# Two transformer layers on one core: the values' split moves to GpSimd, and the accumulator, the query copies and the casts of the second attention are laid out anew

## The chip, the cores and the metric

One Trainium2 chip, one of its cores. The metric is the device time in microseconds (us) of one execution of the whole kernel.

## The reference

Two adaLN blocks run one after the other on x of 2 batches x 512 rows x 512 columns, in fp32. Layer 0 is a sliding window attention with 32 query and 8 key heads and a merged low-rank projection. Layer 1 is the part that matters here: attention with 128 heads of 4 content columns each and a rotary part of 64 columns, then a base projection with 8 low-rank experts.

```python
q_c = (c_q @ Wq_up).reshape(b, s, 128, 4)
q_r = (x @ Wq_rope).reshape(b, s, 128, 64)
k_c = (c_kv @ Wk_up).reshape(b, s, 128, 4)
v_c = (c_kv @ Wv_up).reshape(b, s, 128, 4)
k_r = x @ Wk_rope
scores = (einsum('bqhd,bkhd->bhqk', q_c, k_c) + einsum('bqhd,bkd->bhqk', q_r, k_r)) / scale
attn = softmax(scores, axis=-1)
out = einsum('bhqk,bkhd->bqhd', attn, v_c).reshape(b, s, 512) @ Wo
```

## The kernel before

The five engines run programs written out by hand, which meet only at semaphores. In the second attention the work is cut into 128 **units**: 64 pairs of heads times 2 batches. An even unit is batch 0 of a pair, the odd unit behind it is batch 1 of the same pair. All engines go through **turns** (`period` on ScalarE, VectorE and SyncE, `before_sums` and `behind_sums` on TensorE, `turn` on GpSimd). What one turn u does, in TensorE's order:

- scores 0 to 3 of unit u (two matmuls each, L2551 and L2558), with the maxima products 0 and 1 of unit u+2 between them (L2538)
- `sum_unit(u - 1)`: probabilities times values of the unit before, into bank 7
- scores 4 to 7 of unit u, maxima products 2 to 7 of unit u+2, and the rotary queries of unit u+3 (12 matmuls, L2468 to L2470)

The sums come in two forms. For units below `HALVED` (104) both factors are 16-bit: every probability tile of 128x512 is cast to fp16 and the rest is taken in a second fp16 tile (`halved_part(..., 0)` and `(..., 1)`), and the values are split in three bf16 parts. For three of four key tiles this gives 12 matmuls of 32 columns (L2575), the fourth tile stays fp32 (L2580). From unit 104 on the sums are 8 fp32 matmuls (L2585); this form is called direct here.

What the other engines do in a turn:

- **ScalarE**: the rotary queries' high part from PSUM into `q2` (L1325, L1326), 8 exponentials (L1368), the fp16 casts of tiles 2 to 5 (L1372, L1378), one copy of bank 7 into `ost` (L1364), and the copy of `q2`'s rotary rows into `q1` (`q_high_again`, L1332, L1333).
- **GpSimd** (`halve`): the fp16 casts of tiles 0 and 1 (L879), the six subtractions for the second fp16 tiles, here called the lows (L881, L891), and in every even turn the low part of the rotary weights (L828) between lows 1 and 2.
- **VectorE**: the low part of the rotary queries (L1841, L1842), 8 maxima (L1896), their transpose into `mrow` (L1906), in every even turn the high part of the rotary weights (L1762), and `values`: five small operations on 8 or 24 elements a partition (L1869 to L1878) that split the next unit's values into `vp`.
- **SyncE** issues all transfers of a turn in one fixed order: keys for unit u+1 (L562), keys for the maxima of unit u+3 (L569), content queries of unit u+3 (L573), in even turns rotary weights (L522), four stores of `ost` into `o_d` (L596), and, once VectorE's transpose is there, two small copies of `mrow` into `q2` (L604). Each begins with `hold`, a wait for a semaphore. TensorE's first maxima product of a unit waits for the transfers of L569 and L573 (`mc_loaded`).

SyncE's, ScalarE's, VectorE's and GpSimd's turns run in loops of four turns (`LOOP`, up to turn 101) and are written out before and behind them. TensorE's sums of a unit wait for `p_split` (all six lows), `vp_ready` (the values) and `o_copied` (bank 7 is free).

Of the kernel before, what the change touches and what calls it, by code (L numbers as in the profile page):

```python
# [15 lines left out]
P = 128  # L16
# [19 lines left out]
EARLY = B * (KT - 1)  # L36
TAIL = UNITS - 22
HALVED = TAIL - 2
LOOP = (HALVED - 4) // 4 * 4 + 2
# [5 lines left out]
OROWS = 4 * HD1  # L45
CR = 4 * HD1
SLOTS = [(0, 0), (0, 1), (1, 0), (1, 1), (0, 2), (1, 2), (0, 3), (1, 3)]
HTILES = 3
CONTENT_DMAS = (16, 32)
# [20 lines left out]
def adaln_two_layers(nc, a, out):  # L70
# [4 lines left out]
    o_d = scratch("o_d", (B, H1, 2, OROWS, S))  # L75
# [3 lines left out]
    with ctx:  # L79
# [252 lines left out]
        f_loaded, last_added, f_er_mm, f_er, f_as, fbias_loaded = (sem(n) for n in ("f_loaded", "last_added", "f_er_mm", "f_er", "f_as", "fbias_loaded"))  # L332
# [8 lines left out]
        qr_mm, q2_hi, q1_hi, q1_split = sem("qr_mm"), sem("q2_hi"), sem("q1_hi"), sem("q1_split")  # L341
# [84 lines left out]

        @block.sync
        def _(sp):
# [63 lines left out]
            for k in range(KT):  # L492
# [7 lines left out]
                         .rearrange("p o n -> p (o n)")).then_inc(fbias_loaded, 16)  # L500
# [55 lines left out]
            def period(u, k):  # L556
# [26 lines left out]
                if exists(v, UNITS):  # L583
                    vb = (k + 1) % 2
                    hold(o_copied, v + 1)
                    if not exists(v, DIRECT):
                        for h in range(2):
                            at = HD1 * (2 * (v // 2) + h - H1 + 32)
                            for par in range(2):
                                for dst, r in zip(SUMS[vb], (0, DEN)):  # L590
                                    r += 64 * h + 32 * par
                                    sp.dma_start(dst[at:at + HD1, par], ost[r:r + HD1, vb]).then_inc(sums_loaded[vb], 16)
                    for h in range(2 if exists(v, DIRECT) else 0):
                        for par in range(2):
                            j = 2 * h + par
                            sp.dma_start(o_d[vb, hd(u, k, -1, h), par].rearrange("o c s -> (o c) s"), ost[32 * j:32 * j + OROWS, (k + 1) % 2])\  # L596
                              .then_inc(o_stored[(k + 1) % 2], 16)

                v = u + 2
                if exists(v, UNITS):  # L600
                    hold(m_turned, v + 1)
                    for h in range(2):
                        r = maxrow(h)
                        sp.dma_start(q2[r:r + 1, (k + 2) % 4, h].bitcast(F32).rearrange("p (q n) -> p q n", q=4),  # L604
                                     mrow[h:P:32, k % 2]).then_inc(m_loaded[k % 2], 16)

# [33 lines left out]
            def load_last_sums(b):  # L640

                heads = range(H1 - 32, 2 * (DIRECT // 2))
                sp.wait_ge(o_stored[b], 64 * (DIRECT // 2))
                sp.wait_ge(oo_split, EARLY - 1 + b)
                for par in range(2):
                    for dst, r in zip(SUMS[b], (0, DEN)):
                        sp.dma_start(dst[0:HD1 * len(heads), par], o_d[b, heads.start:heads.stop, par, r:r + HD1]).then_inc(sums_loaded[b], 16)
# [27 lines left out]
            sp.wait_ge(o_copied, UNITS)  # L675
# [22 lines left out]
        def _(pool):  # L698
# [131 lines left out]
            def zero_others():  # L830
# [6 lines left out]
                pool.memset(vp[:, :, HTILES:TB, :, DEN:DEN + HD1], 1.0).then_inc(zeroed, 1)  # L837
                pool.memset(vpb[:, :, 0:HTILES, :, DEN:DEN + HD1], 1.0).then_inc(zeroed, 1)

# [32 lines left out]
            content_low(3)  # L872
            def halve(u, k, pair):

                par = k % 2
                for i in range(2):
                    pool.wait_ge(exp1, 8 * u + 5 + i)
                    pool.sem_inc(spare, 1)
                    pool.tensor_copy(halved_part(par, i, 0), PT[par][:, i]).then_inc(p_split, 1)  # L879
                    pool.wait_ge(p_split, 4 * u + i + 1)  # L880
                    e = pool.tensor_tensor(halved_part(par, i, 1), PT[par][:, i], halved_part(par, i, 0), ALU.subtract)  # L881
                    if i == 1:
                        e.then_inc(p_split, 1)
                if k % 2 == 0:
                    split_rope_weights(pair(4), (k // 2) % 2)
                for i in range(2, 2 * HTILES):
                    if i > 2:
                        pool.wait_ge(exp1, 8 * u + 6 + i)
                    else:
                        pool.wait_ge(exp1, 8 * u + 9)  # L890
                    e = pool.tensor_tensor(halved_part(par, i, 1), PT[par][:, i], halved_part(par, i, 0), ALU.subtract)  # L891
                e.then_inc(p_split, 1)
# [4 lines left out]

            for u in range(6):
                turn(u, u % 4, lambda n, u=u: (u + n) // 2)
# [6 lines left out]
            def load_sums(n, par):  # L906

                b, m = n % 2, n // 2
                if par == 0 and n < B:
                    pool.wait_ge(o_stored[b], 64 * (PAIRS - PAIRS // KT))  # L910
                if par == 0:
                    wait(pool, oo_split, n - 1)
                    wait(pool, o_added, ADDS * n)
                for dst, r in zip(SUMS[b], (0, DEN)):
                    pool.dma_start(dst[:, par], o_d[b, 32 * m:32 * m + 32, par, r:r + HD1]).then_inc(parts_loaded, 16)
                for i in (1, 2):
                    pool.dma_start(sum_parts[2 * par + i - 1], o_d[b, 32 * m:32 * m + 32, par, i * HD1:i * HD1 + HD1]
# [125 lines left out]
        def _(act):  # L1043
# [284 lines left out]
            def q_high_again(z, k):  # L1328

                if exists(z, UNITS):  # L1330
                    act.wait_ge(q2_hi, z + 1)
# [1546 lines left out]
```

## Time and profile before

| what | value |
|---|---|
| three runs | 2184.45, 2190.09, 2193.27 us |
| median | 2190.09 us |
| the profiled execution, its own time | 2190.74 us |
| span of its trace | 2188.9 us |
| mean granted clock of TensorE | 0.995 |
| second attention, turns 6 to 102, a turn | 9.98 us |
| its direct form, a turn | 10.45 us |

The span is the time from the first to the last instruction. A turn's length is the distance from one transpose (L1906) to the next. In the timelines all times are microseconds from the span's start, and a row that ends in "x2" merges two neighbouring instructions, whose starts are closer than their durations where the engine overlaps them.

### The profile page before, as it was taken

The numbers are of one execution on the slowest core, as the hardware profiler recorded it, in microseconds if no ns is written. First come the engines' busy times: TensorE is split into PE (matmuls) and PEld (weight loads), VectorE is DVE, ScalarE is ACT, GpSimd is POOL, SyncE is SP. The second block draws the span as 40 slices with busy tenths as digits, with TensorE's granted clock in tenths as the row PEclk, the third lists the DMA queues.
The fourth block names the chain that finished last, engine by engine and source line by source line (L and its number), as shares of the span: only waits on it lengthen the run. The fifth ranks groups of instructions, "written<-read, shape, count | busy, mean of one in ns | idle before, by whom it ended". The sixth has DMA issues, their size and how long they took to land.

```text
span 2188.9 us, 43788 instructions
## 1 busy us (share of the span) xinstructions
PE 2135.0 (98%) x11308; PEld 1644.0 (75%) x11308; DVE 1814.7 (83%) x3415; ACT 1535.5 (70%) x3060; POOL 1554.4 (71%) x1395
## 2 busy tenths in 40 slices
PE   7999999999999999999999999999999999999978
PEld 4788888888886757777777777777777777777756
DVE  6787787787786758999999999999999998788764
ACT  2443443443434579999999999999999999777742
POOL 4766766766753448888888888889888988455334
PEclk9999999999999999999999999999999999999999
DMA  7011010010013242111111111111111111433341
GB/s 248 24 45 30 20 47 29 19 48 29 19 26 114 56 159 86 47 49 41 49 47 42 48 48 46 42 48 47 49 42 49 47 48 45 124 97 107 86 127 39
DMA packets 125559, 132.17 MB, mean 60 GB/s; under 512 B 33221, under 2 KB 75877, under 8 KB 125492
## 3 DMA queue, kind: packets, MB, share of 16 engines
q1 hardware_dynamic: 121652, 118.77, 18.4%
q0 software_dynamic: 3840, 12.59, 1.9%
q8 instruction: 33, 0.54, 0.1%
q14 instruction: 34, 0.28, 0.0%
HBM read 101.52 MB, written 29.10 MB: 60 GB/s over the span
## 4 chain that ended last, share of the span: by engine, by line
PE 81%; DVE 9%; issue 4%; SPq 2%; DMA 1%; ACT 1%; POOL 1%; DVEq 0%; ACTq 0%; POOLq 0%
PE bank L2538 10%; PE bank L2551 10%; PE bank L2558 9%; PE bank L2115 7%; PE bank L2117 7%; PE bank L2116 7%; PE bank L2470 5%; PE bank L2468 5%; PE bank L2469 5%; PE bank L2575 3%; PE bank L2585 2%; PE bank L2580 2%; DVE mcol L1896 1%; DVE rope_b L1585 1%; DVE rope_a L1584 1%
## 5 line engine op out<-in xcount | busy, mean ns | idle before, releaser
L1896 DVE TENSOR_REDUCE mcol<-bank 128x1 fp32r<-128x512 f32 x1024 | 690.0, 685 | 118.2 <-PE bank L2538 104.8
L2538 PE MATMUL bank<-km,q 128*128 128x512 f32 x1024 | 417.8, 409 | 5.0 <-ACT q L1326 1.6
L2551 PE MATMUL bank<-q,k 128*128 128x512 f32 x1024 | 417.9, 408 | 0.1
L2558 PE MATMUL bank<-q,k 128*128 128x512 f32 x1024 | 404.2, 395 | 0.0
L2538 PEld LDWEIGHTS bank<-km,q 128*128 128x128 f32 x1024 | 317.6, 310 | 71.6 <-DVE mcol L1896 20.3
L1368 ACT ACTIVATE pT<-bank 128x512 f32<-128x512 f32 x512 | 279.5, 599 | 27.6 <-PE bank L2558 23.1
L1368 ACT ACTIVATE x<-bank 128x512 f32<-128x512 f32 x512 | 279.2, 599 | 23.2 <-PE bank L2558 19.0
L2551 PEld LDWEIGHTS bank<-q,k 128*128 128x128 f32 x1024 | 192.3, 188 | 81.8 <-issue 30.2
L2558 PEld LDWEIGHTS bank<-q,k 128*128 128x128 f32 x1024 | 193.5, 189 | 32.3
L2470 PE MATMUL bank<-hT_hi,wr_lo 128*128 128x512 f32 x512 | 205.3, 401 | 0.0
L2468 PE MATMUL bank<-hT_hi,wr_hi 128*128 128x512 f32 x512 | 202.2, 395 | 0.1
L2469 PE MATMUL bank<-hT_lo,wr_hi 128*128 128x512 f32 x512 | 202.3, 395 | 0.0
L2115 PE MATMUL bank<-hT_hi,w_hi 128*128 128x512 f32 x376 | 150.3, 400 | 0.0
L2117 PE MATMUL bank<-hT_hi,w_lo 128*128 128x512 f32 x376 | 148.5, 395 | 0.0
L2116 PE MATMUL bank<-hT_lo,w_hi 128*128 128x512 f32 x376 | 148.4, 395 | 0.0
L722 POOL TENSOR_TENSOR bq_lo<-rope_a,bq_hi 128x512 fp32r<-128x512 f32 x64 | 83.3, 1302 | 82.0 <-ACT bq_hi L1097 82.0
L881 POOL TENSOR_TENSOR pH<-x,pH 128x512 f16<-128x512 f32 x104 | 131.9, 1269 | 8.3
L714 POOL TENSOR_TENSOR rope_a<-rope_a,rope_b 128x512 f32<-128x512 f32 x80 | 106.0, 1325 | 43.4 <-DVE rope_b L1586 43.4
L891 POOL TENSOR_TENSOR pH_late<-pT,pH_late 128x512 f16<-128x512 f32 x104 | 121.6, 1169 | 19.9 <-ACT pT L1368 18.5
L881 POOL TENSOR_TENSOR pH<-pT,pH 128x512 f16<-128x512 f32 x104 | 121.4, 1167 | 8.3
L828 POOL TENSOR_TENSOR wr_lo<-wst,wr_hi 128x512 fp32r<-128x512 f32 x64 | 82.8, 1293 | 56.1 <-DVE wr_hi L1762 56.0
L891 POOL TENSOR_TENSOR pH<-pT,pH 128x512 f16<-128x512 f32 x104 | 119.5, 1170 | 0.3 <-ACT pT L1368 0.2
(375 smaller groups left out, 5402.4 us busy)
## 6 DMA issues: line engine op xcount, KB each, us to landing
wst<-in_L_attn_Wq_rope SPq DMA_DIRECT2D x64, 256.0 KB, 3.0
o_d<-ost SPq DMA_DIRECT2D x504, 32.0 KB, 1.8
st_q<-in_L_attn_wq SPq DMA_DIRECT2D x8, 1024.0 KB, 7.8
st_wo<-in_L_attn_wo SPq DMA_DIRECT2D x8, 1024.0 KB, 5.1
km<-kc_d SPq DMA_DIRECT2D x256, 32.0 KB
q<-qc_d SPq DMA_DIRECT2D x256, 32.0 KB
k<-kc_d SPq DMA_DIRECT2D x256, 32.0 KB
wm<-in_L_wmod SPq DMA_DIRECT2D x6, 1024.0 KB, 10.2
```

The source lines that it names most:

```text
L881: e = pool.tensor_tensor(halved_part(par, i, 1), PT[par][:, i], halved_part(par, i, 0), ALU.subtract)
L1368: act.activation(PT[k % 2][:, s], bank[s % 4][:], ACT.Exp, scale=float((HD1 + ROPE) ** -0.5)).then_inc(exp1, 1)
L1896: dve.tensor_reduce(mcol[:, k % 2, i % 4, i // 4:i // 4 + 1], bank[4 + i % 2][:], AX.X, ALU.max, negate=True)\
L2115: pe.matmul(ps, lh_, rh, start=(i == 0), stop=False)
L2116: pe.matmul(ps, lh_, rl, start=False, stop=False)
L2117: e = pe.matmul(ps, ll, rh, start=False, stop=(i == n - 1))
L2468: pe.matmul(bank[6][:], wr_hi[:, par, kk], hT_hi[:, kk, at], start=(kk == 0), stop=False)
L2469: pe.matmul(bank[6][:], wr_hi[:, par, kk], hT_lo[:, kk, at], start=False, stop=False)
L2470: e = pe.matmul(bank[6][:], wr_lo[:, par, kk], hT_hi[:, kk, at], start=False, stop=(kk == KT - 1))
L2538: pe.matmul(bank[4 + i % 2][:], q2[:, k % 4, h, i % 4:S:4], km[:, b, h], start=True, stop=True).then_inc(max_mm, 1)
L2551: pe.matmul(bank[s % 4][:], k1[:, k % 2, t], q1[:, k % 4, h], start=True, stop=False)
L2558: pe.matmul(bank[s % 4][:], k2[:, k % 2, h, t], q2[:, k % 4, h], start=False, stop=True).then_inc(scores1, 1)
```

## The change

- `values` runs on GpSimd for the units in the 16-bit form: its five operations stand in `halve` between the rotary weights' low part and lows 2 to 5, and each of the last three waits for the one before. VectorE keeps `values` for the direct form alone.
- All six fp16 casts are ScalarE's. `CAST_BEHIND` says behind which exponential each stands: tile 0 behind exponential 1, tile 1 behind 2, tiles 2 and 3 behind 3, tile 4 behind 4, tile 5 behind 5. GpSimd's lows 0 and 1 now wait for exponentials 2 and 3.
- The values of batch 1 stand 16 columns further in `vp`, so that both batches' sums gather in bank 7. It is copied and stored once for a pair (`o_d` has another layout), with one transfer of 128 rows in place of eight of 16 rows.
- `q_high_again` is gone. SyncE copies the rotary rows of `q2` into `q1` by two transfers of 64 rows x 2 KB, issued behind the two of `mrow` and ahead of the next turn's keys.
- `HALVED` is 96, not 104, and `LOOP` 94, not 102: eight more units take the direct form.
- The bias of layer 0 counts on `f_loaded` (10 transfers, not 9).

```diff
+HALVED = EARLY * UNITS // (B * KT)
+LOOP = HALVED - 2
-HALVED = TAIL - 2
-LOOP = (HALVED - 4) // 4 * 4 + 2
+CAST_BEHIND = {1: (0,), 2: (1,), 3: (2, 3), 4: (4,), 5: (5,)}
...
SyncE, period
-                if exists(v, UNITS):
-                    hold(o_copied, v + 1)
...
-                            sp.dma_start(o_d[vb, hd(u, k, -1, h), par].rearrange("o c s -> (o c) s"), ost[32 * j:32 * j + OROWS, (k + 1) % 2])\
+                if exists(v, DIRECT) and k % 2 == 0:
+                    par, pair = (k - 1) // 2 % 2, pairs(u, k, -1)
+                    hold(o_copied, pair + 1)
+                    sp.dma_start(o_d[bass.ds(pair, 1)].rearrange("o h g b c s -> (o h g b c) s"), ost[:, par]).then_inc(o_stored[par], 16)
...
+                    hold(q2_hi, v + 1)
+                    for h in range(2):
+                        r = slice(ROPE * h, ROPE * h + ROPE)
+                        sp.dma_start(q1[r, (k + 2) % 4, h].bitcast(F32), q2[r, (k + 2) % 4, h].bitcast(F32)).then_inc(q1_hi[k % 2], 16)
...
GpSimd
+            def values(v, k, pair):
+                kp = k % 2
+                full = vc[:, TB * kp:TB * kp + TB, bass.ds(pair * 8, 8)].rearrange("p t (h d) -> p t h d", h=2)
+                src = full[:, 0:HTILES]
+                first, second, third = (vpb[:, kp, 0:HTILES, :, OROWS * kp + i * HD1:OROWS * kp + i * HD1 + HD1] for i in range(3))
+                wait(pool, pv1, v - 1)
+                pool.sem_inc(spare, 1)
+                pool.tensor_copy(first, src).then_inc(vp_ready, 1)
+                pool.tensor_copy(vp[:, kp, HTILES:TB, :, OROWS * kp:OROWS * kp + HD1], full[:, HTILES:TB])
+                pool.wait_ge(vp_ready, VP_STEPS * v + 1)
+                pool.sem_inc(spare, 1)
+                pool.tensor_tensor(vrest, src, first, ALU.subtract).then_inc(vp_ready, 1)
+                pool.wait_ge(vp_ready, VP_STEPS * v + 2)
+                pool.sem_inc(spare, 1)
+                pool.tensor_copy(second, vrest).then_inc(vp_ready, 1)
+                pool.wait_ge(vp_ready, VP_STEPS * v + 3)
+                pool.sem_inc(spare, 1)
+                pool.tensor_tensor(third, vrest, second, ALU.subtract).then_inc(vp_ready, 1)
...
-                    pool.tensor_copy(halved_part(par, i, 0), PT[par][:, i]).then_inc(p_split, 1)
...
+                def lows(tiles):
+                    for i in tiles:
+                        pool.wait_ge(exp1, 8 * u + (7, 8, 9, 9, 10, 11)[i])
+                        pool.sem_inc(spare, 1)
+                        e = pool.tensor_tensor(halved_part(par, i, 1), PT[par][:, i], halved_part(par, i, 0), ALU.subtract)
...
+                lows((0, 1))
                 if k % 2 == 0:
                     split_rope_weights(pair(4), (k // 2) % 2)
+                if not (isinstance(u, int) and u == HALVED - 1):
+                    values(u + 1, k + 1, pair(1))
+                lows(range(2, 2 * HTILES))
...
ScalarE
-            def q_high_again(z, k):
...
-                        if exists(u - 1, UNITS):
+                        if exists(u - 1, UNITS) and (k % 2 == 0 or isinstance(u, int) and u - 1 == DIRECT):
...
+                    if s in CAST_BEHIND and exists(u, HALVED):
...
+                        for i in CAST_BEHIND[s]:
+                            act.wait_ge(exp1, 8 * u + 5 + i)
+                            act.activation(halved_part(k % 2, i, 0), PT[k % 2][:, i], ACT.Copy)
...
TensorE, sum_unit
+                    opens, closes = apart or k % 2 == 0, apart or k % 2 == 1
-                                              start=(kb == 0), stop=False)
+                                              start=(kb == 0 and opens), stop=False)
```

## Rows read from the trace of the kernel before

**Rows 1.** The page, part 1: busy time of each engine.

```profile
PE 2135.0 (98%) x11308; PEld 1644.0 (75%) x11308; DVE 1814.7 (83%) x3415; ACT 1535.5 (70%) x3060; POOL 1554.4 (71%) x1395
```

**Rows 2.** One line (L1906), 870 to 1840 us and 1870 to 2080 us: count, min/median/max ns, first and last start.

```profile
L1906 DVE STREAM_TRANSPOSE mrow<-mcol x97: 406/412/424, 876.2 to 1834.1; 128x128 f32<-128x128 f32 x97
...
L1906 DVE STREAM_TRANSPOSE mrow<-mcol x20: 402/410/417, 1873.7 to 2072.3; 128x128 f32<-128x128 f32 x20
```

**Rows 3.** Timeline of TensorE, even turn 62: start, duration, instruction.

```profile
1436.74 0.40 PE L2538 MATMUL bank<-km,q 128*128 128x512 f32 x1
...
1437.54 0.62 PE L2575 MATMUL bank<-pH,vp 128*32 128x512 f16 x8
...
1444.66 0.40 PE L2538 MATMUL bank<-km,q 128*128 128x512 f32 x1
...
1446.52 0.52 PE L2538 MATMUL bank<-km,q 128*128 128x512 f32 x1
...
1456.48 0.62 PE L2538 MATMUL bank<-km,q 128*128 128x512 f32 x1
```

**Rows 4.** Timeline of ScalarE, the same turn.

```profile
1436.31 2.07 ACT L1368 ACTIVATE x<-bank 128x512 f32<-128x512 f32 x4
1438.41 1.15 ACT L1372 ACTIVATE pH<-x 128x512 f16<-128x512 f32 x2
...
1442.29 0.62 ACT L1332 ACTIVATE q<-q 64x512 fp32r<-64x512 f32 x1
```

**Rows 5.** Timeline of GpSimd, the same turn.

```profile
1437.07 0.61 POOL L879 CAST pH<-x 128x512 f16<-128x512 f32 x1 [1.44 <-ACT x L1368]
1437.77 1.16 POOL L881 TENSOR_TENSOR pH<-x,pH 128x512 f16<-128x512 f32 x1
...
1439.56 1.44 POOL L881 TENSOR_TENSOR pH<-x,pH 128x512 f16<-128x512 f32 x1
1440.96 1.29 POOL L828 TENSOR_TENSOR wr_lo<-wst,wr_hi 128x512 fp32r<-128x512 f32 x1
1442.22 2.30 POOL L891 TENSOR_TENSOR pH<-x,pH 128x512 f16<-128x512 f32 x2
1444.47 2.30 POOL L891 TENSOR_TENSOR pH_late<-x,pH_late 128x512 f16<-128x512 f32 x2
```

**Rows 6.** Timeline of VectorE, the same turn.

```profile
1439.55 0.43 DVE L1762 CAST wr_hi<-wst 128x512 fp32r<-128x512 f32 x1
...
1445.61 0.68 DVE L1896 TENSOR_REDUCE mcol<-bank 128x1 fp32r<-128x512 f32 x1
1446.32 0.41 DVE L1906 STREAM_TRANSPOSE mrow<-mcol 128x128 f32<-128x128 f32 x1
```

**Rows 7.** One line (L1870, a copy of 8 elements in `values`), the whole span.

```profile
L1870 DVE COPY vp<-vc x104: 161/730/1187, 807.8 to 1839.2; 128x8 f32 x96, 128x8 f32<-128x8 f32 x8
```

**Rows 8.** Timeline of GpSimd ahead of the second attention: its smallest operations.

```profile
764.87 0.30 POOL L835 MEMSET mcol<- 128x256 f32 x1
765.23 0.11 POOL L837 MEMSET vp<- 128x16 f32 x1
765.28 0.14 POOL L838 MEMSET vp<- 128x48 bf16 x1
```

**Rows 9.** Timeline of SyncE's issues, odd turn 63; then one ahead of the attention.

```profile
1447.26 1.20 SPq L604 DMA_DIRECT2D q<-mrow  x2
1448.85 1.69 SPq L562 DMA_DIRECT2D k<-kc_d  x2
...
1452.70 1.40 SPq L573 DMA_DIRECT2D q<-qc_d  x2
1454.36 1.85 SPq L596 DMA_DIRECT2D o_d<-ost  x4
...
731.77 0.60 SPq L516 DMA_DIRECT2D up<-in_L_attn_Wk_up  x1
```

**Rows 10.** The chain that ended last, in order of time: start, duration, what.

```profile
1482.99 3.21 DMA q<-qc_d
```

More of the change, by code:

```diff
@@ L45 @@
 OROWS = 4 * HD1
+COPIES = PAIRS + 1
 CR = 4 * HD1
@@ L836, in zero_others @@
                 pool.wait_ge(zeroed, 3)
-                pool.memset(vp[:, :, HTILES:TB, :, DEN:DEN + HD1], 1.0).then_inc(zeroed, 1)
-                pool.memset(vpb[:, :, 0:HTILES, :, DEN:DEN + HD1], 1.0).then_inc(zeroed, 1)
+                for kp in range(2):
+                    ones = slice(OROWS * kp + DEN, OROWS * kp + DEN + HD1)
+                    pool.memset(vp[:, kp, HTILES:TB, :, ones], 1.0).then_inc(zeroed, 1)
+                    pool.memset(vpb[:, kp, 0:HTILES, :, ones], 1.0).then_inc(zeroed, 1)
             add_attention(4 * LAST - 1, 3)
@@ L909, in load_sums @@
                 if par == 0 and n < B:
-                    pool.wait_ge(o_stored[b], 64 * (PAIRS - PAIRS // KT))
+                    for i in range(2):
+                        pool.wait_ge(o_stored[i], 8 * (PAIRS - PAIRS // KT))
                 if par == 0:
@@ L1360, in period @@
                     if s == 4:
-                        if exists(u - 1, UNITS):
+                        if exists(u - 1, UNITS) and (k % 2 == 0 or isinstance(u, int) and u - 1 == DIRECT):
+                            i = (k - 1) // 2 % 2 if not (isinstance(u, int) and u == UNITS) else 0
                             act.wait_ge(pv1, u)
-                            wait(act, o_stored[(k + 1) % 2], 64 * pair(-1))
-                            act.activation(ost[:, (k + 1) % 2], bank[7][:], ACT.Copy).then_inc(o_copied, 1)
+                            if isinstance(u, int) and u == UNITS:
+                                act.wait_ge(o_stored[0], 8 * PAIRS)
+                            else:
+                                wait(act, o_stored[i], 8 * (pair(-1) - i))
+                            act.activation(ost[:, i], bank[7][:], ACT.Copy).then_inc(o_copied, 1)
                     if exists(u, UNITS):
@@ L1866, in values @@
[L1866 to L1878 removed]
+                if step == 0:
+                    if v == HALVED:
+                        dve.wait_ge(vp_ready, VP_STEPS * HALVED)
+                    dve.wait_ge(pv1, v - 1)
@@ L1915, in period @@
                 maxima(u + 2, k + 2, pair(2), pair(1), pair(4), quad(4))
-                if not exists(u + 2, UNITS):
+                if not exists(u + 2, UNITS) and HALVED <= u + 1 < UNITS:
                     for step in range(4):
@@ L2564, in sum_unit @@
                     pe.wait_ge(vp_ready, VP_STEPS * w + VP_STEPS)
-                    wait(pe, o_copied, w)
+                    if k % 2 == 0:
+                        wait(pe, o_copied, pair)
+                    elif isinstance(w, int) and w == UNITS - 1:
+                        pe.wait_ge(o_copied, PAIRS)
                     if isinstance(w, int) and w == 0:
@@ L2584, in sum_unit @@
                             h, kb = SLOTS[s]
-                            e = pe.matmul(rows(2 * h + kb % 2), vp[:, k % 2, kb, h], PT[k % 2][:, s], start=(s < 4), stop=(s >= 4))
+                            e = pe.matmul(rows(2 * h + kb % 2), vp[:, k % 2, kb, h], PT[k % 2][:, s], start=(s < 4 and opens), stop=(s >= 4 and closes))
                     e.then_inc(pv1, 1)
```

138 lines of the change are left out of this document (51 added, 87 removed).

## The prediction

> **What bounds the kernel now.** I first read the page's busy times: TensorE works in 98% of the span and no other engine above 83% [rows 1]. So the question in each stage is how much TensorE waits. Then the length of a turn, from the transposes: 96 turns between 876.2 and 1834.1 us are 9.98 us each, 19 turns between 1873.7 and 2072.3 us are 10.45 us each [rows 2]. The first stretch has the 16-bit sums, the second the direct ones. Then the timeline of one even turn: it takes 9.78 us from maxima product 0 to the next one (1436.74 to 1446.52), without a wait on the way. This is TensorE's own work, the floor of a 16-bit turn [rows 3]. A pair of turns is thus 19.56 at the floor and 19.96 as measured: only 0.40 a pair is waiting, some 19 us in all. A change that speeds up other engines can give back no more than that; one that makes TensorE wait has no such bound. The direct turn is 0.47 dearer than the average 16-bit turn.
>
> TensorE's sums start 0.80 behind product 0 (1437.54 against 1436.74), so the sums of unit 62 can start at 1446.52 + 0.80 = 1447.32. GpSimd's last low of unit 62 ends at 1444.47 + 2.30 = 1446.77 [rows 3, 5]. That is the slack to watch: 0.55 us in an even turn, in which GpSimd also does the rotary weights (1.29). In an odd turn it has about 1.3 more.
>
> **The change part by part.**
>
> *ScalarE.* It loses two rotary copies of 0.62 a turn and half the copies of bank 7, and gains two casts of about 0.62 [rows 4]. The load stays. Only the order counts. The four exponentials of a turn start 0.49 apart from 1436.31, a cast takes 0.53 of the queue (two in 1.15). With cast 0 behind exponential 1, exponential 2 starts at 1436.31 + 2 x 0.49 + 0.53 = 1437.8 and ends at 1438.4; exponential 3, one cast later, ends at 1439.4. TensorE needs these banks again only for scores 6 and 7, more than two us later, so the delay costs nothing on that side.
>
> *GpSimd, lows 0 and 1.* The step from an exponential's end (1436.91) to GpSimd's cast (1437.07) is 0.16 [rows 4, 5]. Low 0 therefore starts at 1438.4 + 0.16 = 1438.6, low 1 1.13 behind it (two lows in 2.30), and low 1 ends at 1440.9. Before, GpSimd came to the rotary weights at 1440.96. The two casts that it loses give nothing, since it now starts 1.5 us later: it reaches the rotary weights when it did before.
>
> One row makes this uncertain by a few tenths. Low 1 took 1.44 in place of 1.16 when VectorE's cast of the rotary weights (1439.55, 0.43) began next to it [rows 5, 6]; low 1 will again be near that cast, so I add 0.1. The Trainium skill (SBUF — State Buffer, "Who interferes with whom") states that whichever of the two begins first holds the shared port pair for its whole instruction and blocks the other. The trace agrees, with 0.28 for the low that came second. By that rule alone a low 1 that comes first would hold VectorE's cast back to 1440.9 and the rotary weights to about 1441.4; that would be 0.45 in place of 0.1, and some 16 us more in the result.
>
> *GpSimd, values.* Five small operations are inserted between the rotary weights and the last four lows. The trace has none of their kind there. Its smallest writes take 0.11 (16 elements) and 0.14 (48 elements) [rows 8]; a low of 512 elements takes 1.16, some 2.1 ns an element above 0.1, so 24 elements make 0.15. Three one-input steps of 0.12 and two subtractions of 0.15 are 0.66. Three of them wait for the one before, each with a semaphore step of 0.16 as above, 0.48; with a little for addresses that come from a register, V = 1.2 us. Bounds: 0.55 (five times 0.11, no gap) and 2.0 (five times the 0.30 of a 256-element write plus 0.48). I take 1.2, as the sizes are nearest to the 0.11 and 0.14 rows.
>
> *The stall that follows.* In an even turn the last low ends V + 0.1 later, at 1446.77 + 1.3 = 1448.07; with 0.1 for the signal TensorE could begin the sums at 1448.17, but wants them at 1447.32. Stall S = 0.85 us, in each odd turn. In odd turns GpSimd has no rotary weights and catches up: no stall. Pair: 19.56 + 0.85 = 20.41 against 19.96, so +0.45. Late next are scores 4 and all behind them; nothing gives it back, as every cycle starts anew from TensorE. Units 0 to 95 have 48 even ones, of which the first two lie in the run-in: 46 x 0.45 = +20.7 us.
>
> *VectorE.* It loses the five steps, which often wait (L1870: 0.16 at least, 0.73 in the middle, 1.19 at most) [rows 7]. That removes the 0.40 a pair of waiting; the pair's floor above counts it as gained already.
>
> *Eight more direct units.* 8 x (10.45 - 9.98) = +3.8 us.
>
> *Stores and the accumulator.* One transfer for eight; only SyncE's queue gains. TensorE's number of matmuls is the same.
>
> *Query copies by SyncE.* This part has a cycle of its own. Maxima product 7 starts 7.92 behind product 0. Its transpose ended 2.07 later (1446.73), of which 0.5 was VectorE being late (the last maximum at 1445.61 for a product that ended at 1445.06) [rows 3, 6]. Then SyncE: `mrow`, keys, keys, content queries, 1447.26 to 1454.10 = 6.84, and the next product 0 that needs them starts at 1456.48, 2.38 later [rows 3, 9]. The chain of waits does run over such a transfer, 3.21 from issue to landing [rows 10]. The sum 7.92 + 1.57 + 0.10 + 6.84 + 2.38 = 18.8 spans two turns, against 19.56: 0.75 of slack. The two copies are put in the middle of it: a 64-row load takes 0.60 to issue [rows 9], so 2 x 0.62 + 0.1 for the hold = 1.3. New sum 20.1: above the floor, just under GpSimd's 20.41. It would alone cost 0.15 a pair. The four stores (1.85) lie behind the content queries and not in it. The two cycles mostly hide each other; for turns in which a late landing and a stall at the sums add up I put 0.05 a turn, +4 us over 90 turns.
>
> *Layer 0's bias* lands behind the other transfers that are waited for much later: nothing. The end is unchanged.
>
> Sum: 2190.7 + 20.7 + 3.8 + 4 = 2219.2 for the profiled execution, whose own time is 0.6 above the median of the runs shown (2190.1). **Forecast: 2219 us.**
>
> **Rivals.**
>
> 1. *VectorE's relief wins (faster).* If GpSimd gets through the values within its slack, S = 0 and each pair falls to 19.56: 46 x (-0.40) + 3.8 = -14.6, 2176 us. For it speak VectorE's waits in `values`; against it that the slack is 0.55 and even five operations without any gap take 0.55. The point that decides is S = 0.32, that is V + 0.1 = 0.77. The Trainium skill's rule on the shared port pair (SBUF — State Buffer, same section) is on this rival's side, as VectorE's small copies no longer wait for GpSimd's lows; L1870's 0.16 to 1.19 agrees.
> 2. *Both small: no change.* V between 0.65 and 1.05 with a short issue of the copies gives S of 0.2 to 0.65 and -5 to +15: about 2194.
> 3. *SyncE's cycle is the bound.* If the copies cost 1.0 each to issue, or the content queries land 0.7 later behind 256 KB of copies, the cycle is 20.8 a pair: 46 x 0.84 + 3.8 = +42, 2233; both together 21.5 and 2265.
> 4. *Values on GpSimd much dearer*, V = 2.0: S = 1.65, +61 us, 2252.
>
> **How the numbers follow.** A measurement of this kernel can tell 0.5% (11 us) from no change. Chances: forecast with its neighbourhood (2202 to 2230) 0.44; rival 3 0.16; rival 4 0.12; rival 2 0.16; rival 1 0.12. The range leaves out most of rival 1 and the far ends of 3 and 4: 2187 to 2252. Faster by over 0.5%: 0.12; within: 0.16; slower: 0.72.
>
> **What would show it.** Turns of the 16-bit stretch alternate, with odd ones 0.8 longer in the gap ahead of the first sum matmul, released by GpSimd's last low; GpSimd's five small operations take 1.2 from the first start to the next low; lows 0 and 1 start 1.5 us later than the casts did; VectorE's idle time grows by 2 us a turn; exponential 2 follows cast 0. Wrong would be: GpSimd idle ahead of its lows in even turns, TensorE's wait at product 0 with the content queries' transfer as releaser (rival 3), or turns of 9.78 throughout (rival 1).

## The result and the profile after

The changed kernel takes 2242.18 us (median of 4, 2240.09 to 2244.38), the kernel before, measured beside it, 2190.41. The ratio is 1.024 with a 95% interval of 1.0216 to 1.0264. I had forecast 2219: slower, as said and inside the range, but by 52 us where I had forecast 29. Ratios and intervals below leave out executions in a slower state of the chip: there was one, 2324.30 us in experiment 5 at a granted clock of 0.846, and without it that experiment's median would be 2211.17.

The page of the changed kernel, parts 1 and 4: busy times, then the chain that ended last; below them the same chain in the kernel before.

```profile
PE 2144.8 (96%) x11276; PEld 1644.0 (73%) x11276; DVE 1650.2 (74%) x2903; ACT 1431.8 (64%) x2901; POOL 1461.2 (65%) x1621
...
PE 58%; DVE 9%; SPq 9%; issue 8%; POOL 7%; DMA 5%; ACT 3%; POOLq 0%; ACTq 0%; DVEq 0%
```

```profile
PE 81%; DVE 9%; issue 4%; SPq 2%; DMA 1%; ACT 1%; POOL 1%; DVEq 0%; ACTq 0%; POOLq 0%
```

Every engine but TensorE has become emptier against [rows 1], VectorE by 164 us and GpSimd by 93. TensorE's share of the span fell from 98% to 96%: it waits more. The chain tells more: only 58% of it lies on TensorE, where it was 81%. SyncE's queue (SPq) and the DMAs together have 14% in place of 3, though neither computes anything, and GpSimd has 7% in place of 1.

Next I counted where the 51 us of span are. The transposes of `mcol`, first before (L1906, from 860 to 1776 and from 860 to 2140 us), then after (L1919, from 860 to 1810 and from 860 to 2140), with the same number of turns in each pair.

```profile
L1906 DVE STREAM_TRANSPOSE mrow<-mcol x92: 406/412/424, 866.6 to 1773.8; 128x128 f32<-128x128 f32 x92
L1906 DVE STREAM_TRANSPOSE mrow<-mcol x122: 402/411/424, 866.6 to 2080.9; 128x128 f32<-128x128 f32 x122
```

```profile
L1919 DVE STREAM_TRANSPOSE mrow<-mcol x92: 402/407/416, 866.3 to 1806.7; 128x128 f32<-128x128 f32 x92
L1919 DVE STREAM_TRANSPOSE mrow<-mcol x122: 402/407/416, 866.3 to 2130.1; 128x128 f32<-128x128 f32 x122
```

Both kernels come to 866 us together, so the bias and all before it cost nothing (0.3 us less). The 91 turns behind it take 940.4 in place of 907.2 us: +33.2, 10.33 a turn in place of 9.97. The next 30 take 323.4 in place of 307.1: +16.3, of which 3.8 are the eight units that have changed form. The rest, 12.5, was in no term of mine. The end takes 1.6 more, the start 0.3 less. The sum is 50.8, the difference of the spans.

So two questions are open: what sets 10.33 in the 16-bit turns, and what makes the direct turns dear. The waits of the changed kernel between 870 and 1790 us (total, times, longest) name somebody else than I did:

```profile
DVE mcol L1909 <- PE bank L2551: 231.9, 384, 1.6
...
PEld bank L2551 <- issue: 43.1, 48, 1.8
...
PE bank L2551 <- DMA q<-qc_d: 22.5, 36, 1.4
...
PE bank L2593 <- POOL pH_late L912: 6.0, 19, 0.6
```

The wait that my forecast is built on, TensorE's sums (L2593) for GpSimd's last low, is there only 19 times, with 6.0 us in all. TensorE waits more at L2551, the maxima products, for the content queries. Timeline of TensorE, where one turn meets the next:

```profile
1466.09 0.40 PE L2564 MATMUL bank<-q,k 128*128 128x512 f32 x1
1467.25 0.61 PE L2551 MATMUL bank<-km,q 128*128 128x512 f32 x1 [0.76 <-DMA q<-qc_d]
1467.70 0.40 PE L2571 MATMUL bank<-q,k 128*128 128x512 f32 x1
...
1468.26 0.62 PE L2593 MATMUL bank<-pH,vp 128*32 128x512 f16 x8
```

GpSimd in the same turn:

```profile
1458.38 2.47 POOL L912 TENSOR_TENSOR pH<-x,pH 128x512 f16<-128x512 f32 x2 [2.62 <-ACT x L1398]
1460.81 1.29 POOL L838 TENSOR_TENSOR wr_lo<-wst,wr_hi 128x512 fp32r<-128x512 f32 x1
1462.05 0.20 POOL L893 CAST vp<-vc 128x24 bf16 x1
...
1462.85 0.20 POOL L900 CAST vp<-l_pad 128x24 bf16<-128x24 f32 x1 [0.17 <-POOL l_pad L897]
1463.23 0.24 POOL L903 TENSOR_TENSOR vp<-l_pad,vp 128x24 bf16<-128x24 f32 x1 [0.18 <-POOL vp L900]
1463.43 2.28 POOL L912 TENSOR_TENSOR pH<-x,pH 128x512 f16<-128x512 f32 x2
1465.68 2.27 POOL L912 TENSOR_TENSOR pH_late<-x,pH_late 128x512 f16<-128x512 f32 x2
```

GpSimd ends at 1467.95, the sums start at 1468.26: it is nearly late. But TensorE has come late too, as product 0 began at 1467.25 and not behind 1466.09. And SyncE's issues, the two turns of which this is the middle:

```profile
1456.35 1.19 SPq L609 DMA_DIRECT2D q<-mrow  x2
1457.66 1.17 SPq L614 DMA_DIRECT2D q<-q  x2
1459.62 1.78 SPq L569 DMA_DIRECT2D k<-kc_d  x2
1461.79 1.59 SPq L576 DMA_DIRECT2D km<-kc_d  x2
1463.56 1.37 SPq L580 DMA_DIRECT2D q<-qc_d  x2
...
1466.51 1.22 SPq L609 DMA_DIRECT2D q<-mrow  x2
```

Read against [rows 9], the two copies (L614, 1.17) stand between `mrow` and the keys, and the content queries (L580) have been issued 8.58 us behind `mrow`'s first issue (1456.35 to 1464.93), where [rows 9] have 6.84. The chain of the changed kernel between 1455 and 1468 us goes over all of it: VectorE's last maximum, its transpose, each issue of SyncE, the transfer, product 0.

```profile
1455.13 0.70 DVE mcol L1909
1455.85 0.41 DVE mrow L1919
...
1464.29 2.83 DMA q<-qc_d
...
1467.25 0.61 PE bank L2551
```

Rival 3 thus has the trace on its side. The experiments are to tell whether it has the time too.

### The profile page after: what moved, and what is told of

Same layout as the page of the kernel before. It is cut to its first block, busy times and chain, and to the rows that moved or that the text cites. A ratio compares the mean times of both kernels' runs of the same rounds, so it can differ in the third digit from the quotient of the medians.

```text
span 2239.7 us, 42472 instructions
## 1 busy us (share of the span) xinstructions
PE 2144.8 (96%) x11276; PEld 1644.0 (73%) x11276; DVE 1650.2 (74%) x2903; ACT 1431.8 (64%) x2901; POOL 1461.2 (65%) x1621
## 4 chain that ended last, share of the span: by engine, by line
PE 58%; DVE 9%; SPq 9%; issue 8%; POOL 7%; DMA 5%; ACT 3%; POOLq 0%; ACTq 0%; DVEq 0%
PE bank L2128 6%; PE bank L2130 6%; PE bank L2129 6%; PE bank L2551 6%; PE bank L2564 5%; PE bank L2571 5%; DMA q<-qc_d 3%; PE bank L2483 3%; PE bank L2481 3%; PE bank L2482 3%; POOL pH L912 2%; SPq L569 2%; POOL pH_late L912 2%; PE bank L2603 2%; PE bank L2593 2%
## 5 line engine op out<-in xcount | busy, mean ns | idle before, releaser
L2551 PE MATMUL bank<-km,q 128*128 128x512 f32 x1024 | 417.5, 409 | 30.5 <-DMA q<-qc_d 22.5
L2564 PE MATMUL bank<-q,k 128*128 128x512 f32 x1024 | 418.2, 408 | 7.6 <-DMA k<-kc_d 7.6
L2551 PEld LDWEIGHTS bank<-km,q 128*128 128x128 f32 x1024 | 317.6, 310 | 99.2 <-issue 48.7
L1398 ACT ACTIVATE pT<-bank 128x512 f32<-128x512 f32 x512 | 296.5, 600 | 143.9 <-PE bank L2571 134.0
L1398 ACT ACTIVATE x<-bank 128x512 f32<-128x512 f32 x512 | 295.7, 599 | 56.3 <-PE bank L2571 54.1
L912 POOL TENSOR_TENSOR pH<-x,pH 128x512 f16<-128x512 f32 x192 | 228.9, 1212 | 128.2 <-ACT x L1398 128.2
L2564 PEld LDWEIGHTS bank<-q,k 128*128 128x128 f32 x1024 | 192.3, 188 | 94.1 <-issue 44.0
L912 POOL TENSOR_TENSOR pH<-pT,pH 128x512 f16<-128x512 f32 x192 | 220.1, 1167 | 10.8 <-ACT pT L1398 10.7
L1405 ACT ACTIVATE pH<-x 128x512 f16<-128x512 f32 x192 | 117.2, 643 | 0.0
L1405 ACT ACTIVATE pH<-pT 128x512 f16<-128x512 f32 x192 | 117.1, 641 | 0.0
```

What stands on the lines that cost most here:

```text
L1398: act.activation(PT[k % 2][:, s], bank[s % 4][:], ACT.Exp, scale=float((HD1 + ROPE) ** -0.5)).then_inc(exp1, 1)
L2551: pe.matmul(bank[4 + i % 2][:], q2[:, k % 4, h, i % 4:S:4], km[:, b, h], start=True, stop=True).then_inc(max_mm, 1)
L2564: pe.matmul(bank[s % 4][:], k1[:, k % 2, t], q1[:, k % 4, h], start=True, stop=False)
```

## The experiments

Gaps below are from the starts of neighbouring matmuls of the trace, as means over the even or the odd ones of units 6 to 91; without any wait product 0 follows 0.235 behind the matmul before it, and the sums 0.33 behind theirs. Product 0 and the sums of the unit before stand in the same turn. In the changed kernel both are late in odd turns, and nearly in these alone: product 0, which comes right after an even turn's last matmul, follows after 0.905 (+0.67), the sums after 0.49 (+0.16). A pair of turns is 20.65.

**1. Values back on VectorE**, all else as in the changed kernel.

```diff
 GpSimd, halve
-                if not (isinstance(u, int) and u == HALVED - 1):
-                    values(u + 1, k + 1, pair(1))
 VectorE, values, behind maxima 3 to 6
+                if exists(v, HALVED):
+                    if step == 0:
+                        wait(dve, pv1, v - 1)
+                        dve.tensor_copy(first, src).then_inc(vp_ready, 1)
+                        dve.tensor_copy(vp[:, kp, HTILES:TB, :, cols], full[:, HTILES:TB])
...
```

> The changed kernel with the values' split back on VectorE for all units; all else as changed. Theory A (SyncE's two-turn cycle, lengthened by the query copies, is what sets the 16-bit turns: 10.33 us in the changed kernel's trace) expects no gain, since the cycle stays and VectorE's transpose comes up to 0.5 us later again: 2242 to 2255 us. Theory B (the five operations on GpSimd make TensorE wait at the sums, the step that the prediction priced highest) expects the stall to go: some 20 us back, 2222 us.

2255.32 us, ratio 1.0296 (1.0261 to 1.0332). Taking my stall away makes the kernel slower still. The gap ahead of the sums is 0.33 in every turn, so GpSimd's stall, 0.16 a pair in the changed kernel, is gone. It did not carry the loss. The longest wait of TensorE's matmuls in this kernel, 870 to 1790 us, is for the queries:

```profile
PE bank L2541 <- DMA q<-qc_d: 32.9, 52, 1.7
```

VectorE, full again (81%), ends its transpose 2.0 to 2.2 us behind product 7, where the changed kernel has 1.57, and that stands at the head of SyncE's cycle. So this experiment takes one wait out of the cycle and puts a longer one in; it does not show what GpSimd's stall alone is worth there.

**2. Query copies back on ScalarE**, all else as in the changed kernel.

```diff
 SyncE, period
-                    hold(q2_hi, v + 1)
-                    for h in range(2):
-                        r = slice(ROPE * h, ROPE * h + ROPE)
...
 ScalarE, period, ahead of exponential 6
+                        q_high_again(u + 2, k + 2)
```

> The changed kernel with the rotary query copies back on ScalarE, none by SyncE; the values stay on GpSimd. Theory A pure expects the 16-bit turns near the floor, 9.85 us, and the direct stretch back at 10.45: 2242 - 43 - 11 = 2188 us. Theory B expects that almost nothing changes in the 16-bit stretch. If both waits lie side by side (A and B as two cycles of nearly the same length), GpSimd's stall comes out from behind SyncE's: with V = 1.4 us from the trace S is about 1.05, the turn 10.3, and only the direct stretch's 11 us come back: 2231 us.

2231.73 us (1.0192, 1.0168 to 1.0215). The direct turns are back at 10.45, but the 16-bit turns are not shorter (10.35). Odd turns now show GpSimd's stall (gap ahead of the sums 0.85, +0.52), and product 0 in the same turns still comes 0.39 late. The content queries are not the cause, as they land 1.23 ahead of it in the mean. The trace names ScalarE's copy of the rotary queries' high part (L1356), for which product 0 waits too:

```profile
1466.69 0.62 PE L2555 MATMUL bank<-km,q 128*128 128x512 f32 x1 [0.28 <-ACT q L1356]
```

All 43 odd turns wait, and product 0 starts 0.19 behind the end of that copy in the mean; in even turns, without a wait, it starts 0.46 behind. ScalarE, which makes six casts and the two copies here, is late.

**3. The order of two issues.** SyncE still makes the copies, but behind the content queries in place of ahead of the keys. A wait for the turn's own first scores goes with them.

```diff
 SyncE, period
                 if k % 2 == 0:
                     load_rope_weights(pairs(u, k, 6), (k // 2 + 3) % 2)
+                v = u + 2
+                if exists(v, UNITS):
+                    hold(scores1, 8 * (v - 2) + 1)
+                    hold(q2_hi, v + 1)
+                    for h in range(2):
...
 behind the two transfers of mrow
-                    hold(q2_hi, v + 1)
-                    for h in range(2):
...
```

> The changed kernel with the two query copies still by SyncE, but issued behind the content queries and rotary weights of the same turn (with one more hold for the slot), so out of the cycle from transpose to maxima product 0. Load of queues and transfers is the same. Theory A expects the same as for the copies on ScalarE; if two cycles lie side by side, 2231 us; if it is not the order but the transfers themselves that disturb (traffic), 2242 us as changed.

2224.91 us (1.0157, 1.0129 to 1.0184): 17.3 less than the changed kernel, for the place of two transfers. And now my stall is in full view. TensorE in this kernel, then GpSimd's last two lows, which end ahead of it at 1465.16:

```profile
1465.30 0.62 PE L2596 MATMUL bank<-pH,vp 128*32 128x512 f16 x8 [0.94 <-POOL pH_late L915]
```

```profile
1462.87 2.29 POOL L915 TENSOR_TENSOR pH_late<-x,pH_late 128x512 f16<-128x512 f32 x2
```

In the waits (870 to 1790 us) the two causes have changed places:

```profile
PE bank L2596 <- POOL pH_late L915: 39.4, 44, 1.0
...
PE bank L2554 <- DMA q<-qc_d: 0.2, 1, 0.2
```

Even turns are 9.80, odd ones 10.77, with a gap of 1.29 ahead of the sums: S = 0.96 (0.85 predicted). The transposes of this kernel, from 860 to 1810 and from 1810 to 2140 us:

```profile
L1922 DVE STREAM_TRANSPOSE mrow<-mcol x92: 402/404/414, 866.5 to 1802.9; 128x128 f32<-128x128 f32 x92
...
L1922 DVE STREAM_TRANSPOSE mrow<-mcol x30: 402/407/418, 1812.4 to 2114.2; 128x128 f32<-128x128 f32 x30
```

The 91 turns take 936.4 in place of 940.4, only 4 us less: GpSimd's cycle (20.56 a pair) lay just under SyncE's (20.65), and takes over as soon as that is gone. The larger part of the gain, 12 us, comes from the 30 turns behind them: 311.3 (1802.9 to 2114.2), where the changed kernel has 323.4.

What goes on there: in the changed kernel GpSimd loads the gathered sums of the direct stretch, eight transfers of 256 KB in a row, and SyncE's content queries are issued in the middle of them. GpSimd, SyncE, TensorE:

```profile
1894.32 0.71 POOL L949 DMA_DIRECT2D num<-o_d  x1
...
1898.15 1.50 POOL L951 DMA_DIRECT2D vc<-o_d  x2
```

```profile
1895.61 1.29 SPq L580 DMA_DIRECT2D q<-qc_d  x2
```

```profile
1903.75 0.78 PE L2551 MATMUL bank<-km,q 128*128 128x512 f32 x1 [3.04 <-issue]
```

Product 0 starts 6.85 behind the end of that issue, where [rows 3, 9] have 2.38. The waits of TensorE from 1810 to 2080 us in the changed kernel:

```profile
PE bank L2564 <- DMA k<-kc_d: 4.7, 4, 1.6
...
PE bank L2551 <- issue: 3.0, 1, 3.0
```

With the copies behind, the same issue runs from 1890.40 to 1891.69 against a first load at 1890.43, and TensorE's matmuls wait 0.2 us in all for transfers and issues in that stretch. The turn with the loads is 15.3 us long in the changed kernel and 10.4 here, so this is 4.9 of the 12 us. The rest lies in five later turns, each third one: 12.1 to 12.8 us in the changed kernel, 10.9 to 11.5 here, and in each of the five TensorE waits for keys (L2564, 6.1 us in all).

The kept traces agree that what counts is how the issue lies to GpSimd's loads. Where it begins with the first load, the transfer lands 3.97 to 4.69 us behind the issue's end (the kernel before, experiments 2 to 5 and 11). Where it begins 1.3 to 5.6 us later, that is 5.06 to 8.18 (the changed kernel, experiments 1 and 6 to 10). In the turns up to 91 it is 2.3 to 2.5 in the mean. Experiments 9 and 10, with 5.47 and 6.33, have no copy by SyncE in that turn, so the copies' traffic is not needed for it. I have not moved the loads themselves.

**4. Both at once:** values on VectorE and copies behind (the edits of 1 and 3).

> Both at once: values back on VectorE and the copies behind the content queries. If the two cycles together explain the loss, the 16-bit turn falls to 9.85 to 9.98 us and the direct stretch to 10.45: about 2192 us, with the eight more direct units' 4 us still in it. If something else costs (casts 0 and 1 late, the shared accumulator), it stays above 2205 us.

2204.1 us (1.0061, 1.0038 to 1.0084). Alone, the two edits gave -17.3 and +13.1; together they give -38. So each of the two cycles hides the other. It is 12 us above the 2192 that I expected, and close to the 2205 above which something else was to cost. What is left against before is 14 us. By the traces 5.8 of it lie in the 91 turns (913.0 against 907.2) and 5.8 in the 30 behind them (312.9 against 307.1), of which the eight units were priced at 3.8. I have not taken the rest apart. VectorE is as full as before (83%), and the waits of TensorE's weight loads for its maxima are 20.6 us between 870 and 1790, where the kernel before has 15.4.

**5. Values on GpSimd alone**, in the kernel before: its casts, copies, stores and HALVED.

```diff
 GpSimd, halve, behind the rotary weights' low part
+                if not (isinstance(u, int) and u == HALVED - 1):
+                    values(u + 1, k + 1, pair(1))
 VectorE, values
+                if not isinstance(v, int) or v < HALVED:
+                    return
```

> The kernel before with one part of the change alone: the five operations of the values' split on GpSimd, between the rotary weights' low part and lows 2 to 5. Theory A (GpSimd's chain of an even turn ends behind the point at which TensorE wants the sums): V = 1.4 us against a slack of 0.55, less 0.2 for the signal, gives a stall of about 1.05 in each odd turn and turns of 9.78 and 10.8; 50 pairs of 20.6 in place of 19.96 make +32 us, 2222 us. Rival (VectorE's relief is worth more, or GpSimd's lows run faster without it): 2175 to 2190 us.

2212.64 us (1.0104, 1.0077 to 1.0131). Here the mechanism of my forecast is alone, and it is as described: even turns 9.80, odd turns 10.50, a gap of 1.00 ahead of the sums (+0.68, where the expectation had 1.05 and so 9 us too much), released by GpSimd:

```profile
PE bank L2604 <- POOL pH_late L913: 27.2, 43, 0.7
```

**6. Copies by SyncE alone**, in the kernel before, with its four stores a turn. The bias's transfer counts on `f_loaded` here too.

```diff
 SyncE, period, behind the transfers of mrow
+                    hold(q2_hi, v + 1)
+                    for h in range(2):
...
 ScalarE, period
-                        q_high_again(u + 2, k + 2)
```

> The kernel before with one part alone: ScalarE's two rotary copies of a turn replaced by SyncE's two transfers behind those of mrow; the four stores of a turn stay, ScalarE casts four tiles. Theory A: SyncE's queue has no room: its issues of a pair of turns take about 19.3 us of 19.96, and four copies of 0.65 make 21.9; the 16-bit turn grows to about 10.95 us, +95 us, 2285 us. Rival (only the two-turn cycle counts, with the latency and not the load of the queue): cycle 18.8 + 1.3 + 0.5 for the late transposes and 0.4 for the stores, turns of 10.5, +52 us, 2242 us.

2288.33 us (1.0446, 1.0424 to 1.0468): the dearest of all. SyncE in this kernel:

```profile
1454.90 1.22 SPq L605 DMA_DIRECT2D q<-mrow  x2
1456.24 1.17 SPq L610 DMA_DIRECT2D q<-q  x2
1457.77 1.74 SPq L563 DMA_DIRECT2D k<-kc_d  x2
1459.88 1.61 SPq L570 DMA_DIRECT2D km<-kc_d  x2
1461.66 1.38 SPq L574 DMA_DIRECT2D q<-qc_d  x2
1463.42 1.86 SPq L597 DMA_DIRECT2D o_d<-ost  x4
1465.49 1.20 SPq L605 DMA_DIRECT2D q<-mrow  x2
```

There is hardly a gap in it (0.38 us at most). A turn's issues fill 10.6 us, more than TensorE's 9.8, so SyncE is the bound here, while the page's part 1 does not list it. Two more things show it: the queue waits for VectorE's transpose 5 times between 870 and 1790 us, 3.2 us in all, where the changed kernel has 66 times and 120.7 us; and `mrow` is issued some 1.0 us behind the transpose's end, not 0.1 to 0.3. The single store of the change takes this load off: two times 1.86 for four stores against one of 0.44 make 3.3 us a pair. So I estimate that without it the changed kernel would have been bound by SyncE's queue too, which I did not run. "Only SyncE's queue gains" was then a line of much worth.

**7 and 8. The rotary weights' low part to VectorE**, to give GpSimd its 1.29 back; on top of experiment 3. In 8 HALVED is 104 as well.

```diff
 GpSimd, split_rope_weights
-                if exists(p, PAIRS):
+                if False:
 VectorE, period, behind maximum 3 of even turns
+                        if i == 3 and k % 2 == 0:
+                            rope_weights_low(p, (k // 2 - 1) % 2)
 (8 only)
-HALVED = EARLY * UNITS // (B * KT)
+HALVED = 104
```

> The changed kernel with the copies behind the content queries, and the rotary weights' low part moved from GpSimd to VectorE (behind the fourth maximum of an even turn), where the values' split has left room. If what is left of the loss in the 16-bit stretch is GpSimd's even turn alone (1.02 us a pair in the trace of the run with the copies behind), both turns fall to 9.78: 2225 - 46 = 2179 us. Rival (the two-input subtraction on VectorE waits for GpSimd's lows and holds up the maxima, or another wait lies 0.2 to 0.4 behind): 2190 to 2200 us.

> The same with 104 units in the 16-bit form, as in the kernel before. Eight turns of 9.78 in place of 10.45: 5.4 us less than with 96, 2174 us if the run with 96 gives 2179. Rival: no difference, if the run-out of the 16-bit form meets the gathering of the sums.

2194.49 us (1.0019, 1.0001 to 1.0036) and 2190.01 (1.0002, 0.9985 to 1.0019). The first is 30.4 below experiment 3; it missed the 2179 that I expected by 15, and the rival had it. By the traces the 91 turns gain 36.4 (900.0 against 936.4), as GpSimd's stall is gone but for 0.13 in odd turns, and the 30 behind them lose 5.9 (317.2 against 311.3). Turns are 9.83 and 9.95, but behind unit 97 single ones of 11.2 to 12.7 stand next to the gathering. The eight units are worth 4.5 (3.8 predicted).

**9 and 10.** Experiment 8 with ScalarE's copies in the direct form; and that with casts 0 and 1 one exponential earlier.

```diff
 (9) SyncE
-                if exists(v, UNITS):
+                if exists(v, HALVED):
 (9) ScalarE, period, for units from HALVED on
+                        q_high_again(u + 2, k + 2)
 (10 only)
-CAST_BEHIND = {1: (0,), 2: (1,), 3: (2, 3), 4: (4,), 5: (5,)}
+CAST_BEHIND = {0: (0,), 1: (1,), 3: (2, 3), 4: (4,), 5: (5,)}
-                        pool.wait_ge(exp1, 8 * u + (7, 8, 9, 9, 10, 11)[i])
+                        pool.wait_ge(exp1, 8 * u + (6, 7, 9, 9, 10, 11)[i])
```

> The last kernel (values on GpSimd, rotary low part on VectorE, copies behind the content queries, 104 units) with the rotary copies of the units from 104 on made by ScalarE again, so that no copy by SyncE runs beside the gathering of the sums. In that kernel's trace the direct turns lie 5.3 us in all above 10.45, in single turns of 11.4 to 11.8 next to the gathering. If the copies' transfers cause this, 2190 - 5 = 2185 us and all direct turns at 10.45. Rival (the single stores of 256 KB or GpSimd's loads alone cause it): no change.

> The same, with casts 0 and 1 right behind exponentials 0 and 1, so that GpSimd's lows 0 and 1 wait for exponentials 1 and 2 and start some 0.35 us earlier. In the trace of the last kernel odd turns are 9.95 with 0.12 to 0.17 us of waiting ahead of the sums, even ones 9.77. If GpSimd's late start is what is left, odd turns fall to 9.78 and the kernel by 0.17 x 48 = 8 us, to 2177 us. Rival (exponentials 1 to 3 come later and hold the scores, or the wait is VectorE's): no gain, 2185 us or more.

2187.31 us (0.9986, 0.9971 to 1.0) and 2185.29 (0.9969, 0.9955 to 0.9983). Experiment 9 is 2.7 below experiment 8, but the two ratios' intervals overlap, and of the 4.1 us between the traces' spans only 2.1 lie in the last 30 turns, the only ones that the edit changes. The direct turns did not come to 10.45 as expected: those next to the gathering are still 11.1 to 12.2, so the copies' traffic is not all that makes them long. Experiment 10 is the best kernel here, 0.3% faster than before. Its sums follow after 0.33 in every turn: GpSimd's stall is gone, and the 91 turns take 894.7 in place of 900.0. But the turn with GpSimd's loads grew from 12.0 to 14.5, so that 2.0 of the 8 us that I expected are left.

**11. Casts 0 and 1 back on GpSimd**, on top of experiment 3.

```diff
-CAST_BEHIND = {1: (0,), 2: (1,), 3: (2, 3), 4: (4,), 5: (5,)}
+CAST_BEHIND = {3: (2, 3), 4: (4,), 5: (5,)}
 GpSimd, halve
-                lows((0, 1))
+                for i in range(2):
+                    pool.wait_ge(exp1, 8 * u + 5 + i)
+                    pool.sem_inc(spare, 1)
+                    pool.tensor_copy(halved_part(par, i, 0), PT[par][:, i]).then_inc(p_split, 1)
+                    pool.wait_ge(p_split, 3 * u + i + 1)
+                    pool.tensor_tensor(halved_part(par, i, 1), PT[par][:, i], halved_part(par, i, 0), ALU.subtract)
```

> The changed kernel with the copies behind the content queries (2225 us), and casts 0 and 1 back on GpSimd. The prediction held that GpSimd gains nothing from losing these casts, because it starts later by the same time. The odd turns are 10.53 in the run with the values alone and 10.79 in the run with the copies behind, so the move of the casts would cost 0.26 a pair: odd turns of 10.53 and 2213 us. Rival (the difference lies in the waits that each low now has, or in the accumulator): 2225 us.

2212.16 us (1.01, 1.0073 to 1.0127): 12.7 below experiment 3, the stall now 0.63 in place of 0.96. Taking work *off* GpSimd had cost 12.7 us. GpSimd's even turn in both kernels says why, as its lows now wait for ScalarE's casts: in experiment 3, as in the changed kernel, it stands idle for 2.62 us ahead of its first low; here it does not wait at all:

```profile
1465.51 0.61 POOL L922 CAST pH<-x 128x512 f16<-128x512 f32 x1
...
1468.00 1.23 POOL L924 TENSOR_TENSOR pH<-x,pH 128x512 f16<-128x512 f32 x1
1469.18 1.29 POOL L841 TENSOR_TENSOR wr_lo<-wst,wr_hi 128x512 fp32r<-128x512 f32 x1
```

## Why the prediction was right in sign and short in size

**The step that failed** is the sum of SyncE's cycle: "New sum 20.1: above the floor, just under GpSimd's 20.41", and what followed from it, "The two cycles mostly hide each other; ... +4 us". The parts of the change were priced well: two copies with their hold 1.3, as measured, and SyncE's 6.84 is just its mean in the kernel before. What was small was the rest of the cycle, and it has to be read where it binds. Of the turns 6 to 91 all 43 odd ones wait at product 0, which starts 0.13 to 0.23 behind the landing of the content queries; of the even ones two do. (A sum over all turns would prove nothing: the steps of a closed cycle add up to its length whether it binds or not.) From an odd turn to the next odd one, in the mean, the way from product 0 to product 7 was 8.31, not 7.92; from there to the end of the transpose 1.56, as taken; then 0.10 to `mrow`; SyncE's part 8.19 against 8.14, with 8.58 in every fourth turn, where its loop begins anew, as in the timeline above; and product 0 came 2.48 behind that, not 2.38. This is 20.64, where the terms of the forecast add up to 20.11. Of the 0.53 between them 0.39 lies in TensorE's own part: 0.16 is the wait at the sums for GpSimd, which lies *on* this cycle, and 0.2 is that the matmul behind a late product 0 comes late too. So the two waits did not hide each other: in odd turns they stand one behind the other. A pair is 20.65 in place of 19.96: +0.70, 46 times, +32 us, where I had +25. Rival 3, to which I gave 0.16, has the mechanism. Its own price (20.8, +42) was nearer than mine, though its reason, copies at 1.0 each or a later landing, was not the true one.

**GpSimd's stall** was the right mechanism in the wrong place. Experiments 3 and 5 show it, odd turns only, released by the last low, 0.96 and 0.68 long. In the changed kernel most of it lies behind TensorE's wait for the queries, and 0.16 a pair is left. What that costs there is open, since experiment 1, which takes it away, also delays the transposes. Its size was a little low too. V is 1.38 (1462.05 to 1463.43), not 1.2: operations of 24 elements take 0.20 to 0.24, not 0.12 to 0.15. The 0.11 and 0.14 of [rows 8] were memsets, which read nothing. The gaps between dependent steps, 0.17 and 0.18, were right.

**"The two casts that it loses give nothing"** overlooked that they cost something. I had the lows start 1.5 later and the rotary weights when they did before. In the changed kernel GpSimd goes idle for 2.62 first, and experiment 11 prices the move at 12.7 us, 0.28 a pair, with the copies behind.

**"The end is unchanged" and the direct form at its old price.** The direct stretch lost 12.5 us that no term had. Experiment 3 shows that the place of the copies does it, as 12.1 come back. They push the content queries 1.3 later: 4.9 us are the one turn in which these fall among GpSimd's eight loads, the rest are later turns with waits for keys.

**ScalarE's own work** was free as said on TensorE's side: even turns come from product 0 to product 7 in 7.94, where the forecast had 7.92. **VectorE's relief** was as forecast: its wait for the maxima products grew by 2.0 us a turn (231.9 us against 52.0 between 870 and 1790), and the transpose came on time. **The eight units** were 3.8 predicted and 4.5 measured. **The accumulator and the single store** gain nothing in the sum, but compare experiments 6 and 1, which both have the values on VectorE and the copies ahead of the keys: without the single store the loss is 98 us, with it 65, though ScalarE's casts and the eight units are in the 65.

**Low 1 beside VectorE's cast.** Both got longer: the cast took 0.80 in the median (L1788, 427/797/804 ns) where [rows 6] have 0.43, and low 0 and 1 together 2.47 for 2.28. The Trainium skill (SBUF — State Buffer, "Who interferes with whom") says that the one which comes first holds the shared port pair and the other is fully blocked. The trace agrees in that it was now the cast that was held back: it began at 1459.03 beside a low that had begun at 1458.38. The 0.45 that I derived from it did not come, as the cast was done before GpSimd asked for its result. In experiment 10 GpSimd's last operation of `values` began 0.03 behind VectorE's two-input subtraction of 0.68, and took 0.75 in place of 0.24. The two rows of its timeline, GpSimd's and VectorE's:

```profile
1451.78 0.75 POOL L906 TENSOR_TENSOR vp<-l_pad,vp 128x24 bf16<-128x24 f32 x1 [0.18 <-POOL vp L903]
```

```profile
1451.75 0.68 DVE L1805 TENSOR_TENSOR wr_lo<-wst,wr_hi 128x512 fp32r<-128x512 f32 x1
```

The same section says that a VectorE instruction with two SBUF inputs contends with a GpSimd instruction that reads SBUF; the trace agrees.

**The account** of +51.8, one edit after the other from the changed kernel: the place of the copies 17.3 (experiment 3), the rotary weights' low part off GpSimd 30.4 (7; of the same stall the casts' move alone is worth 12.7, by 11), the eight units 4.5 (8). This is 52.2, and ends at the time of the kernel before. It holds in this order only, and the whole of it was not undone: experiment 7 gives GpSimd other room than it had before. What GpSimd's part is worth with the copies where they are was not run without loading VectorE again. Open too is whether GpSimd's loads themselves or all the traffic at that moment delay the queries, and why keys come late in the turns behind them.

## What to carry to other kernels

An engine that only issues transfers has a busy time too, and no page shows it: add up its issues over a turn, and follow the cycle that goes through it over several turns, with the turns in which its loop branches and with every other wait that lies on it, before calling a sum "just under" another. That it binds is shown by the wait at its end, and not by the sum of its steps. Where two cycles of nearly the same length bound a kernel, an experiment that undoes one of them alone shows little (here -17 and +13 us), and both together much more (-38). And a transfer that nobody waits for soon is issued behind the one that somebody waits for: 17 us here, for moving two transfers.

## What the hardware showed that I had not expected

- GpSimd's operations of 24 elements a partition take 0.20 to 0.24 us, and 0.17 to 0.18 lie between dependent ones: five of them, 1.38 us, cost more than a subtraction of 512 elements (1.17).
- SyncE's queue is full with 14 issues a turn, and one more in even turns: at 0.46 to 0.87 us each and what lies between them they fill 10.6 us (experiment 6).
- The same content-query transfer was used by TensorE 2.4 us behind its issue in a quiet turn and 6.85 us behind it when GpSimd issued eight loads of 256 KB around it.
- After a wait at product 0 the next matmul follows after 0.45 us in place of 0.235 (1467.25 to 1467.70 in the timeline above; 0.451 to 0.461 in the 42 late ones of the changed kernel among units 6 to 91), so each such stall costs 0.2 us more than the gap that the wait shows.
